# Routing of the two expert parts moved chunk by chunk into the parts ahead of them, and the linear part made one block

## The reference

```python
# moe0, moe1: top 2 of 8 experts for every token (H = 128, F = 512)
xn     = layernorm(x)
logits = xn @ gate_w (+ gate_b)
top2, who = top_k(logits, 2);  share = softmax(top2)
x = x + sum_j share[j] * expert[who[j]](xn)
# linear: attention without a softmax over keys; with q, k, v = xn @ Wq + bq, ... it folds into one 128x128 map
x = x + xn + gamma * (attention of q, k) applied to v        # = x + xn @ M + row
```

## Time and profile before

| | |
|---|---|
| median of 3 runs | 1487.93 us (1487.58 to 1488.09) |
| the profiled execution | 1485.52 us, span 1483.8 us |
| mamba's last DVE instruction ends | 345.28 us |
| moe0: first instruction, first slot tile loaded | 346.49 us, 410.83 us |
| linear: first instruction, last `X` written | 517.46 us, 571.18 us |
| moe1: first instruction, first slot tile loaded | 571.94 us, 637.66 us |
| granted clock of TensorE, mean | 0.884 |

### The profile page before, as it was taken

One profiled execution on the slowest core, in us unless ns is written; L12 is line 12 of the kernel. 1 busy time (PEld: TensorE's weight loads), 2 busy tenths in 40 slices (PEclk: granted clock), 3 DMA queues, 4 the chain that ended last, 5 costly groups with the idle time before them and its releaser, 6 DMA issues. The chain is left out here.

```text
span 1483.8 us, 25208 instructions
## 1 busy us (share of the span) xinstructions
PE 1128.5 (76%) x8381; PEld 725.9 (49%) x8381; DVE 886.7 (60%) x2933; ACT 693.0 (47%) x1261; POOL 560.6 (38%) x712
## 2 busy tenths in 40 slices
PE   8876777785088466079945999959983799979999
PEld 3322222344078454079943677733332577744545
DVE  3599999965345534345558888843645777850110
ACT  2785566642044300022225888737653788642221
POOL 6188988832624311634335323010006655200000
PEclk9899999996589855579976999989995899989999
DMA  2998000004122205111120000020000000020000
GB/s 57 175 193 122 0 0 1 1 1 135 48 61 58 88 3 175 43 52 46 39 83 5 2 2 3 2 45 1 0 1 9 2 2 3 2 82 0 15 0 14
DMA packets 80455, 58.31 MB, mean 39 GB/s; under 512 B 14043, under 2 KB 69221, under 8 KB 80326
## 3 DMA queue, kind: packets, MB, share of 16 engines
q1 hardware_dynamic: 74630, 45.20, 14.5%
q0 software_dynamic: 4544, 9.38, 1.8%
q10 hardware_dynamic: 1152, 2.10, 0.4%
HBM read 28.13 MB, written 28.52 MB: 38 GB/s over the span
## 5 line engine op out<-in xcount | busy, mean ns | idle before, releaser
L912 POOL TENSOR_TENSOR hC<-h,Cs 128x1024 f32<-128x1024 f32 x64 | 150.8, 2357 | 47.9 <-DVE h L824 47.7
L653 PE MATMUL bank<-hC,ident 128*128 128x512 f32 x256 | 130.3, 633 | 49.3 <-POOL hC L912 47.2
L824 DVE TENSOR_TENSOR_SCAN h<-bank,state,dBx 128x512 f32<-128x512 f32 x128 | 157.2, 1270 | 3.7 <-POOL dBx L905 1.7
L1116 POOL DMA_INDIRECT moe_answers<-moe_yw,moe_xg x78 | 83.8, 1075 | 135.7 <-DVE moe_yw L1386 77.3
L2216 DVE CUSTOM_DVE_ANT_0 decay_below<-bank,decay_q_mask 128x256 bf16<-128x256 f32 x256 | 97.6, 419 | 20.1 <-PE bank L2029 19.3
L2216 DVE CUSTOM_DVE_ANT_0 window_below<-bank,window_q_mask 128x192 bf16<-128x192 f32 x256 | 80.5, 353 | 39.3 <-PE bank L2029 37.6
L653 PEld LDWEIGHTS bank<-hC,ident 128*128 128x128 f32 x256 | 45.5, 195 | 111.0 <-POOL hC L912 72.5
L741 ACT ACTIVATE bank<-dt,A 128x512 f32<-128x512 f32 x128 | 83.2, 683 | 28.5 <-DVE h L824 27.4
L1228 PE MATMUL bank<-moe_xgT,moe_wac 128*128 128x128 f32 x624 | 87.4, 286 | 6.5 <-issue 4.1
L2156 ACT ACTIVATE decay_pb<-bank 128x512 f32<-128x512 f32 x128 | 76.2, 598 | 33.9 <-PE bank L2044 33.3
L165 POOL TENSOR_TENSOR rstd<-veps,mhalf 128x4 f32<-128x4 f32 (+1 forms) x14 | 23.1, 1653 | 181.9 <-DVE veps L140 181.9
(11 more groups left out here) (461 smaller groups left out, 2877.9 us busy)
## 6 DMA issues: line engine op xcount, KB each, us to landing
moe_slots<-blank SPq DMA_DIRECT2D x16, 1040.0 KB, 17.7
moe_xg<-moe_slots SPq DMA_DIRECT2D x78, 65.0 KB, 1.8
moe_wa<-in_moe_w SPq DMA_DIRECT2D x2, 2048.0 KB
moe_back<-moe_answers SPq DMA_DIRECT2D x8, 256.0 KB, 5.3
moe_back<-moe_answers ACTq DMA_DIRECT2D x8, 256.0 KB, 6.0
moe_wu<-in_moe_wu SPq DMA_DIRECT2D x1, 2048.0 KB
deep_w<-in_deep_w SPq DMA_DIRECT2D x3, 512.0 KB, 5.2
moe_answers<-moe_yw,moe_xg POOLq DMA_INDIRECT x78
```

The source lines that it names most:

```text
L653: last = nc.tensor.matmul(sum_bank(hh)[:], k.ident[:], hC[:, u % 2, hh, :], start=(n == 0), stop=(n == NS - 1))
L824: v.tensor_tensor_scan(h[:, u % 2, hh, :], decay_bank(u, hh)[:], dBx[:, u % 2, hh, :], state[:, n, hh:hh + 1], ALU.mult, ALU.add).then_inc ...
L912: g.tensor_tensor(hC[:, u % 2], h[:, u % 2], Cs[:, u % 2, None, :].to_broadcast([P, H, CW]), ALU.mult).then_inc(q_hC, 1)
L1116: nc.gpsimd.indirect_dma_start(answers, bass.IndirectOffsetOnAxis(index, 0), yw[:, i % NY, :], None)\
```

## The change

A class `Routing` now holds the tiles, semaphores and steps of the routing, and is made before the part ahead of the experts. Its steps are those of before, with a layer norm for each chunk (`stats`, `power`, `normalise`) in place of the two sweeps. `mamba` calls, inside its feed-forward tail, all of chunk 0 (with 4 of its 8 scatters), and of chunk 1 the norm, the transposition and the logits; also the statistics of chunk 2. `moe0` starts with the other 4 scatters of chunk 0. `linear` takes in chunk 0's norm, transposition and logits, and chunk 1's statistics and power. It is one block now, its bias row is spread over all partitions by a product with the spread bias `bvw`, and DVE adds it to `X` (`add_bias`) where PE had 16 products with the ones. Two tiles of `mamba` (`diag`, `Bs`) lie in memory of `taps_w`, and `bd` counts as a weight now.

```diff
 # mamba, PE
                 for f in range(FB):
+                    if (c, f) == (3, 3):
+                        r.ranks(pe, 0)
                     wait(pe, f_ev, (c - 1) * FB + f + 1)
...
                 for i in range(CT):
+                    if (c, i) == (1, 1):
+                        r.turn(pe, 0)
+                    if (c, i) == (1, 3):
+                        r.gate(pe, 0)
+                    if (c, i) == (3, 2):
+                        r.turn(pe, 1)
...
                 down(c)
+            r.gate(pe, 1)
 # mamba, ACT
                 if c + 2 < C:
                     take_turned(c + 2)
+                if c == 1:
+                    r.take_turned(act, 0)
+                    r.exponentials(act, 0)
+            r.take_turned(act, 1)
 # mamba, DVE
-            for c in range(C):
-                add_ffn(c)
+            r.prepare(dve)
+            add_ffn(0)
+            dve.wait_ge(f_cp, 1)
+            r.stats(dve, 0)
+            r.normalise(dve, 0)
+            r.choose(dve, 0)
+            add_ffn(1)
+            r.slots_of(dve, 0)
+            dve.wait_ge(f_cp, 2)
+            r.stats(dve, 1)
+            add_ffn(2)
+            r.normalise(dve, 1)
+            dve.wait_ge(f_cp, 3)
+            r.stats(dve, 2)
+            add_ffn(3)
 # mamba, POOL
+            r.power(pool, 0)
+            r.power(pool, 1)
+            r.scatter(pool, 0, 0, CT // 2)
+            r.power(pool, 2)
 # experts, POOL
-                k.norm_pool()
...
+                if first:
+                    r.scatter(pool, first - 1, CT // 2, CT)
+                for c in range(first, C):
+                    r.scatter(pool, c, 0, CT // 2)
+                    if c + 2 < C:
+                        r.power(pool, c + 2)
+                    r.scatter(pool, c, CT // 2, CT)
 # experts, ACT
+                for c in range(first, C):
+                    r.exponentials(act, c)
                     if c + 1 < C:
-                        take_turned(c + 1)
-                    exponentials(c)
+                        r.take_turned(act, c + 1)
 # experts, PE
+                for c in range(first, C):
+                    r.ranks(pe, c)
                     if c + 1 < C:
...
+                        r.turn(pe, c + 1)
+                        r.gate(pe, c + 1)
 # experts, DVE
+                for c in range(first, C):
+                    r.choose(dve, c)
+                    if c == C - 1:
+                        v.nop().then_inc(r.s_pick, 1)
                     if c + 1 < C:
...
+                        r.normalise(dve, c + 1)
+                    r.slots_of(dve, c)
+                    if c + 2 < C:
+                        r.stats(dve, c + 2)
 # linear, PE
-                nc.tensor.matmul(bank[5][0:1, 0:P], bv[:], H[:], start=True, stop=True).then_inc(s_m, 1)
+                pe.wait_ge(s_bv, 1)
+                nc.tensor.matmul(bank[5][:, 0:P], bvw[:], H[:], start=True, stop=True).then_inc(s_m, 1)
+                pe.wait_ge(s_M, 1)
+                for c in range(C):
+                    if c >= 2:
+                        pe.wait_ge(s_x, c - 1)
+                    if c == C - 1:
+                        r.turn(pe, 0)
+                    for i in range(CT):
+                        a = (c * CT + i) * P
+                        last = nc.tensor.matmul(bank[c % 2][:, i * P:(i + 1) * P], k.xnT[:, a:a + P], M[:], start=True,
+                                                stop=True)
+                    last.then_inc(s_o, 1)
+                r.gate(pe, 0)
 # linear, DVE
+                r.prepare(dve)
+                add_bias(0)
+                for c in range(C):
+                    if c + 1 < C:
+                        add_bias(c + 1)
+                    dve.wait_ge(s_o, c + 1)
+                    dve.wait_ge(s_xb, c + 1)
+                    v.tensor_tensor(tiles_of(c), bank[c % 2][:].rearrange("p (i d) -> p i d", i=CT), tiles_of(c), ALU.add)\
+                        .then_inc(s_x, 1)
+                    if c < 2:
+                        dve.wait_ge(s_x, c + 1)
+                        r.stats(dve, c)
+                    if c == 1:
+                        r.normalise(dve, 0)
```

More of the change, by code:

```diff
@@ L625, in scan_sync @@
             k.fill(sp)
+            r.load(sp)
         def scan_tensor(pe):
@@ L980, in experts @@
+def experts(k, r, first):
     nc, t, C, T, E = k.nc, k.t, k.C, k.T, k.E
-    L0, bank, pre = k.L, k.bank, name
+    bank, name, pre, gated = k.bank, r.name, r.name, r.gated
     F = t[pre + "_w1"].shape[2]
@@ L1031, in experts @@
         back = sb("back", [P, C, 2, CT, P])
[L1033 to L1036, removed]
+        s_w, s_v, s_table = sem("weights"), sem("table_steps"), sem("table")
         weights = [(wa[:], t[pre + "_w1"].rearrange("e p f -> p e f"))]
@@ L1099, in _ @@
             def _(pool):
-                k.norm_pool()
[L1101 to L1109, removed]
-                            nc.gpsimd.indirect_dma_start(slots, bass.IndirectOffsetOnAxis(index, 0), rows[j][:, i, :], None)\
-                                .then_inc(s_sent, 16)
+                if first:
[5 more added lines that the diff above has]
+                    r.scatter(pool, c, CT // 2, CT)
                 for i in range(NT):
@@ L1316, in _ @@
-                for j in range(2):
-                    v.tensor_copy(rows[j][:, :, P].bitcast(U32), k.token[:, j, :]).then_inc(s_id, 1)
-                step(v.memset(before[:, 0], 0.0))
-                k.norm_stats(0)
-                k.norm_rows(L0, 0, keep=rows[0])
-                k.norm_stats(1)
-                if not gated:
-                    dve.wait_ge(g_w, 16 * len(gates))
-                k.norm_rows(L0, 1, keep=rows[0])
-                choose(0)
-                slots_of(0)
-                for c in range(1, C):
-                    if c + 1 < C:
-                        k.norm_rows(L0, c + 1, keep=rows[0])
-                    choose(c)
-                    if c == C - 1:
-                        v.nop().then_inc(s_pick, 1)
-                    slots_of(c)
@@ L1418, in _, with linear @@
                     onto_x(c)
[L1419 to L1422 removed]
+    r.tmp.close()
+def linear(k, r):
     nc, t, C, T = k.nc, k.t, k.C, k.T
@@ L2880, in program @@
             if part == "mamba":
-                mamba(k)
+                routing = Routing(k, "moe0", gated=False)
+                mamba(k, routing)
+            elif part == "linear":
+                routing = Routing(k, "moe1", gated=True)
+                linear(k, routing)
             elif part in ("moe0", "moe1"):
-                experts(k, part, gated=(part == "moe1"))
-            elif part == "linear":
-                linear(k)
+                k.part_sems += routing.sems
+                experts(k, routing, first=(1 if part == "moe0" else 0))
             elif part in ("decay", "window"):
```

321 lines of the change are left out of this document (192 added, 129 removed).

## The result

The changed kernel took 1440.31 us (median of 4 runs, 1438.41 to 1443.5), the kernel before on the same chip 1488.01 us: ratio 0.9679, 95% interval 0.9659 to 0.9699. That is 47.7 us less, where 31.0 were forecast. The profiled execution was the longest of the four, 1443.5 us (span 1441.8), 42.0 us less than the profiled one of before.

What follows compares the result with a forecast made beforehand. POOL's scatters, with a late start and gaps, were taken to bound both routings, and PE linear's second block. Mamba +3.5, moe0 -18.5, linear -9.1, moe1 -6.9 sum to -31.0: 1487.9 to 1456.9 us, range 1443 to 1473.

Steps and rivals of the forecast that it cites:

- Mamba's tail, +3.5: End of mamba: added routing work makes it 3.5 us longer, POOL finishing last; bounds 1 and 8.
- the 4 us by the exclusive lock: Mamba's four scatters could each wait out a DVE normalisation, some 4 us; the forecast instead went by 0.5 together.
- Gaps of 7 and 8 us: POOL's idle time for late slot numbers: 7 us in moe0 (bounds 0, 14), 8 in moe1 (0, 16).
- Chunk 3's choose starts near 17, after about 13 scatters, so in the crawl.: moe0: choose begins about 17 us in and will not finish until POOL runs dry at 27.
- the crawl: Routings: DVE's steps slow by about 1.45 us each beside a long scatter row, ending about 3 us after POOL runs dry.
- 7 to 10 scatters: Both routings: length of unbroken scatter row after which DVE's slow steps were said to begin.
- the chunk before: moe0 before the change: chunk said to take 3.6 us for the ten DVE steps that took 18.1 in chunk 3.
- 45.8: moe0's routing, border to first slot load, in us, including a gap of 7; 64.3 before, so 18.5 less.
- the load would be late by much the same: moe0: without a POOL gap, DVE's table steps would be slow instead, delaying the slot load about equally.
- The two terms without their gaps, 38.8 and 50.8: Routing sums of moe0 (45.8 with 7 us of gaps) and moe1 (58.8 with 8), border to first slot load.
- Linear, -9.1: Linear: dropping 32 of 64 PE instructions at 0.36 us, less new waits and gate, saves 9.1 us; bounds 11 and 6.
- the powers break the row, and the crawl does not come: Rival for both routings: POOL's powers prevent DVE's slow steps, both gaps go, 15 us less, 1442; chance 0.14.

Runs made afterwards that it cites:

- at_home_third: Changed kernel with moe0's whole routing inside moe0, chunk by chunk, nothing of it in mamba; third run, on a chip with slow steps: 1455.65 us, ratio to before 0.9789.
- lin_wide_row: Kernel before, linear still two blocks with PE's bias row, but from 128 rows of ones against the row divided by 128: ratio 0.9918, linear 40.7 us.
- after_wide_row: Changed kernel with linear's bias row given back to PE, with 128 rows of ones, and taken from DVE: ratio to before 0.9691, linear 43.1 us.
- lin_two_dve_bias: Kernel before, linear still two blocks, but DVE adds the bias row and the one-row products are gone: ratio 0.9881, linear 33.6 us.

## Why the prediction was wrong

1440.3 us lies 2.7 us below the range (1443 to 1473), and 16.7 us more were saved than forecast. The gaps of moe0 (6.9) and moe1 (4.4) and linear (4.0) make up 15.3 of them by the traces. By the prediction's own steps:

1. *Mamba's tail, +3.5:* +3.2, and on all chips 26.9 to 27.1 us against 23.8. POOL is the last, its power(2) ends at 353.11. PE waited for nothing. The scatters beside DVE's normalisation (348.43, 1.15 us long) start at 348.54, 349.81 and 351.07, so at the old pace; the 4 us by the exclusive lock of the Trainium skill ("SBUF — State Buffer", section "SBUF: two separate sides") are not seen. In which mode the normalisation ran, no view tells, so the rule itself is not tested.
2. *The +5.2 us in front of it* are not the change's. For the unchanged scan of the kernel before and its variants, the first `down` stood anywhere from 322.7 to 327.4 us; for the changed kernel from 322.7 to 327.9. The profiled execution of the changed kernel lies 3.2 us above its median and that of the kernel before 2.5 below, which is why the medians show 47.7 and the two traces 42.0.
3. *Gaps of 7 and 8 us: this is the step that failed.* "Chunk 3's choose starts near 17, after about 13 scatters, so in the crawl." It counted the scatters on across POOL's powers, and that count was wrong: in the changed kernel the slow steps show in moe0 after 15 scatters behind the border, in moe1 after 19, and in moe0 of at_home_third after 20, with no head start for DVE. By then chunk 3's slot numbers were all but done, and POOL had no gap for them in either part. The rule had also been misread from its rows: "7 to 10 scatters" is 12 at 379.62, the place given for moe0, and "the chunk before" with its 3.6 us is chunk 1, since chunk 2 already holds the late wait before 377.27. That explains moe0 (45.8 - 7 = 38.8, measured 38.9) and 3.5 us of moe1's 4.4, where 8 us of gap went and 4.5 came back at the table. The prediction had named that mechanism (without a gap the table crawls, and "the load would be late by much the same"); it held in part in moe1 and not in moe0, where the table was done 1.9 us before the last scatter ended. The two terms without their gaps, 38.8 and 50.8, are what the quiet chips show with memsets in POOL's row (39.0 and 50.3): the rest of the sum was right.
4. *Linear, -9.1: mis-sized, -13.1.* It took 0.36 us for the price of an instruction, of whatever kind, because the rows showed only the mixture. The 128-row product has 0.21 at that clock and 0.11 at the other. PE needed 4.18 us for the first 24, not 8.7; then DVE became the bound and gave 4.0 us back as idle time.
5. *The reading of the crawl as a fact of the kernel* was wrong too. It is there on some chips only. The kernel before takes 12 to 14 us longer there, of which the traces show 10 in the two routings; the rest has no explanation here. The changed kernel loses nothing in moe0 (38.9 to 39.1 us against 39.0 with memsets on a quiet chip) and 1.6 to 4.4 us in moe1 (51.9 to 54.7 against 50.3). So the change was worth 47 to 49 us where it exists. On quiet chips only versions with breaks in POOL's row ran; with memsets it was 1473.8 - 1436.0 = 37.8.

The rival "the powers break the row, and the crawl does not come" had the time, 1442, and half the mechanism: the gaps went, the slow steps came, later. That its time fits is in part luck: the 4.5 us that came back at moe1's table are not in it, and neither are the 4.0 us that linear gave on top.

Why the slow steps come later stays open. In the twelve routings with powers in POOL's row that were profiled where they exist, the first wait that quiet chips don't have begins 8.2 to 9.6 us after the last power ends. In the four of the kernel before, whose powers end 7 us or more ahead of the row, it shows 7.4 to 10 us after the first scatter. That is what one would see if a row began anew at each power (memsets did not do it). But DVE's steps always lie in the same place behind the last power, so this agreement is no proof, and the two kernels made to decide it ran on quiet chips.

## What to carry to other kernels

Read the price of an instruction from rows where its kind runs alone: a mixture's mean says nothing of what is left when one kind goes, and one-row products beside 128-row ones are dear. Where one engine's dependent steps lie beside a long row of GpSimd's scatters, order them so that each result is ready well before it is needed. Here slow steps then cost 2 to 4 us in place of 12 to 14, and the time depended less on the chip. Profile the kernel before on the chip of the experiment before explaining a stall by its code.

## What the runs showed of the hardware, unexpected

- The same program has chains of dependent DVE steps at 0.2 to 0.5 us a step on three chips and up to 1.4 (and single waits of 4 to 7) on others, beside indirect scatters on POOL. The kernel before differs by 13 us in its median (1474 and 1487), and 10 of it are in the two routings; other stages of the traces agree within about 1 us, the scan aside.
- A one-row product between 128-row ones: 0.36 us an instruction against 0.213 at the same granted clock (0.50), and the clock did not rise in 24 us of busy PE. With 128 rows everywhere it rose 5.1 and 5.5 us after the first product with M (lin_wide_row, after_wide_row), and after 2.6 and 3.1 us where DVE added the row (the changed kernel, lin_two_dve_bias).
- A memset of 128x4 between two scatters costs POOL nothing: 0.12 us in the 0.30 that stand between two of them, and the pace stays 1.27 us.
